# Another order of the first three batch steps, and of two tile turns, in a cross-attention and sparse FFN kernel

## The reference, cut to what matters

```python
# x: (32, 64, 512), ctx: (32, 64, 512)
# attention, 8 heads of 64, on the normalized x; the context is both key and value
qh = softmax(einsum('bcn,oc->bon', q, Wq).reshape(b, 8, 64, n), axis=-2) * 64 ** -0.5
kh = softmax(einsum('bcn,oc->bon', k, Wk).reshape(b, 8, 64, n), axis=-1)
vh = einsum('bcn,oc->bon', v, Wv).reshape(b, 8, 64, n)
context = einsum('bhdn,bhen->bhde', kh, vh)
out = einsum('bhde,bhdn->bhen', context, qh)
out = einsum('bcn,oc->bon', out.reshape(b, 512, n), Wo) + bo
x = x + out / max(norm(out, axis=1), 1e-12) * g * sqrt(64)
# feed-forward on the normalized rows of x
inter = xf @ c1_w.T @ c2_w.T                       # 1792 columns, 56 blocks of 32
idx = argmax over each block                       # one row of w1 and w2t for each block
h = relu(einsum('bkm,bm->bk', w1[idx], xf))
x = x + einsum('bk,bkm->bm', h, w2t[idx])
```

## Time and profile before

| | |
|---|---|
| median of 3 runs | 772.08 us (771.66 to 772.16) |
| the profiled execution | 771.59 us, span 769.8 us |
| PE busy | 753.8 us (98%) |
| DVE busy | 612.9 us (80%) |
| POOL busy | 476.9 us (62%) |
| ACT busy | 405.0 us (53%) |
| mean granted PE clock | 0.993 |

### The profile page before, as it was taken

How to read it: one execution, slowest core, us unless ns; L and a number is a source line. 1 busy time by engine, 2 the same in 40 slices (tenths; PEclk the granted TensorE clock), 3 DMA queues, 4 the chain that set the end, 5 groups by cost and what they waited for, 6 DMA issues and landing times.

```text
span 769.8 us, 13685 instructions
## 1 busy us (share of the span) xinstructions
PE 753.8 (98%) x4792; PEld 552.9 (72%) x4792; DVE 612.9 (80%) x936; ACT 405.0 (53%) x804; POOL 476.9 (62%) x547
## 2 busy tenths in 40 slices
PE   7979999999999999999999999999999999999998
PEld 6556655665665666666578888888888888888886
DVE  6879999999999999999866667776668766677763
ACT  4869999999999999999721111111111111111110
POOL 3699999988888889977444335544345443355431
PEclk8999999999999999999999999999999999999999
DMA  6143343333323333221111011110111100111000
GB/s 164 49 118 108 103 117 110 102 94 98 101 77 100 93 86 116 85 83 28 35 28 38 5 41 42 42 42 8 34 42 42 42 25 17 42 42 42 27 2 27
DMA packets 30531, 48.04 MB, mean 62 GB/s; under 512 B 4736, under 2 KB 13568, under 8 KB 30464
## 3 DMA queue, kind: packets, MB, share of 16 engines
q1 hardware_dynamic: 29808, 46.45, 20.3%
q10 hardware_dynamic: 656, 0.72, 0.3%
HBM read 38.77 MB, written 8.39 MB: 61 GB/s over the span
## 4 chain that ended last, share of the span: by engine, by line
PE 78%; POOL 13%; DVE 4%; ACT 2%; issue 2%; DMA 1%; DVEq 0%; SPq 0%; POOLq 0%; ACTq 0%
PE po L954 20%; PE slot L926 19%; PE po L1044 9%; PE turn L1029 5%; PE turn L1012 5%; POOL Q L415 5%; PE slot L1070 4%; PE slot L1084 4%; PE turn L939 3%; POOL weights_lo L366 2%; PE slot L911 2%; PE po L1055 2%; POOL c_low L400 2%; POOL x_low L356 1%; POOL weights_hi L364 1%
## 5 line engine op out<-in xcount | busy, mean ns | idle before, releaser
L325 POOL TENSOR_TENSOR E<-E,rank 128x256 bf16<-128x256 bf16 (+1 forms) x64 | 66.6, 1041 | 157.2 <-DVE E L498 157.2
L415 POOL TENSOR_TENSOR Q<-Q,qrec 128x1024 f32<-128x1024 f32 x64 | 121.2, 1903 | 37.7 <-DVE qrec L629 37.3
L1044 PE MATMUL po<-E,ctxT 128*64 128x512 f32 x256 | 116.7, 598 | 0.0
L1047 PE MATMUL po<-QT,G 128*64 128x512 f32 x256 | 116.7, 598 | 0.0
L734 ACT ACTIVATE wk_hi<-turn 128x256 fp32r<-128x256 f32 (+1 forms) x32 | 15.7, 490 | 155.3 <-PE turn L939 155.3
L926 PE MATMUL slot<-weights_hi,c_high 128*128 128x512 f32 (+1 forms) x256 | 96.9, 378 | 0.0
L926 PE MATMUL slot<-weights_hi,c_low 128*128 128x512 f32 (+1 forms) x256 | 94.3, 368 | 0.0
L926 PE MATMUL slot<-weights_lo,c_high 128*128 128x512 f32 (+1 forms) x256 | 94.3, 368 | 0.0
L773 ACT ACTIVATE E<-slot,neg_kmax 128x512 f32<-128x512 f32 x128 | 86.2, 685 | 12.1 <-DVE neg_kmax L615 11.9
L954 PE MATMUL po<-weights_hi,x_high 128*128 128x512 f32 x224 | 88.1, 393 | 0.0
L581 DVE TENSOR_REDUCE qmax<-slot 128x16 f32<-128x1024 f32 x64 | 75.4, 1218 | 14.1 <-PE slot L1084 14.1
(11 more groups left out here) (118 smaller groups left out, 1717.6 us busy)
## 6 DMA issues: line engine op xcount, KB each, us to landing
c_in<-in_ctx SPq DMA_DIRECT2D x64, 128.0 KB, 2.6
x_in<-in_x SPq DMA_DIRECT2D x64, 128.0 KB, 2.5
stage<-in_ffn_w SPq DMA_DIRECT2D x32, 225.0 KB, 2.6
attn_out<-po_sb SPq DMA_DIRECT2D x32, 128.0 KB, 2.3
ctxT<-in_ctxT SPq DMA_DIRECT2D x31, 128.0 KB, 2.1
attn<-attn_out SPq DMA_DIRECT2D x8, 256.0 KB, 3.0
x<-in_x SPq DMA_DIRECT2D x8, 256.0 KB, 2.8
E<-attn_out SPq DMA_DIRECT2D x8, 256.0 KB, 3.8
```

The source lines that it names most:

```text
L415: nc.gpsimd.tensor_tensor(half, half, qrec[1 - par][:, s, :].unsqueeze(2).broadcast_to([P, HALF, D]), ALU.mult).then_inc(q_scaled, 1)
L1044: nc.tensor.matmul(po[0:C, :], ctxT[1 - par][:, m, :], E[1 - par][:, :, m * P:(m + 1) * P], start=(m == 0), stop=(m == NT - 1)).then_inc(p ...
L1047: nc.tensor.matmul(po[C:P, :], G[:, m, :], QT[m][:], start=(m == 0), stop=(m == HT - 1)).then_inc(out_mm, 1)
```

## The change

It does seven things.

1. POOL, step 2: `bias(3, 1)` moves from the end of step 1 to behind the split of the context, and the two weight pieces move behind the scaling of the queries.
2. DVE, step 0: `statistics(1, 1)` moves from ahead of `max_k(1)` to behind `shift_q(0)`.
3. DVE, step 0 to 1: `sum_q(0, 0, 0)` moves behind the first `max_k(0)` of step 1.
4. ACT, step 0: `exp_q(0)` moves ahead of the copies, `norm_x` behind `copy_e(2)`, `exp_q(1)` ahead of `copy_e(3)`.
5. PE, step 0: 4 more matmuls on zeros behind `fold_vo`, and 5 between `queries(0)` and `queries(1)`.
6. PE: `turn_back(0)` moves from the end of step 30 to behind the keys of step 31.
7. `turn_x(0)` writes the bank `turn[1]` in place of `pre`, and waits for three copies of step 31, not four; ACT's and DVE's readers of it take the bank as an argument.

```diff
@@ gpsimd, step
-                    split_items()
+                    if known == 2:
+                        bias(3, 1)
+                    else:
+                        split_items()
...
                     if known == 1:
                         bias(2, 0)
-                    if known > 0:
+                    elif known == 2:
+                        split_items()
+                    if known > 1:
                         bias(g + 2, par)
@@ vector, step
                     max_k(0)
+                    if known == 1:
+                        sum_q(0, 0, 0)
                     invert_q(0)
                     if known == 0:
                         split_first_x()
-                        statistics(1, 1)
                     max_k(1)
...
                     if known == B:
-                        xT_rest(0, 0)
+                        xT_rest(0, 0, turn[1])
...
                     if known == 0:
                         shift_q(0)
+                        statistics(1, 1)
                     max_q(1)
...
-                    sum_q(g, par, 0)
+                    if known != 0:
+                        sum_q(g, par, 0)
@@ scalar, step
                     if known == B:
-                        xT_round(0, 0)
+                        xT_round(0, 0, turn[1])
...
+                    if known == 0:
+                        exp_q(0)
                     copy_e(0)
                     copy_e(1)
-                    if known == 0:
-                        norm_x()
                     copy_q(0)
                     copy_q(1)
                     copy_e(2)
-                    if known == 1:
+                    if known in (0, 1):
                         norm_x()
-                    exp_q(0)
+                    if known != 0:
+                        exp_q(0)
...
+                    if known == 0:
+                        exp_q(1)
                     copy_e(3)
-                    exp_q(1)
+                    if known != 0:
+                        exp_q(1)
@@ tensor
-                def turn_x(a, par):
+                def turn_x(a, par, bank):
                     pe.wait_ge(x2_normed, a + 1)
                     pe.wait_ge(added, a + 1)
                     if a == 0:
-                        pe.wait_ge(q_copied, HT * (B - 1))
+                        pe.wait_ge(q_copied, HT * (B - 2) + 3)
                     for m in range(MT):
-                        last = nc.tensor.transpose(pre[:, m * P:(m + 1) * P], work[:, m * P:(m + 1) * P], ident[:])
+                        last = nc.tensor.transpose(bank[:, m * P:(m + 1) * P], work[:, m * P:(m + 1) * P], ident[:])
                     last.then_inc(x_turned, 1)
...
+                def zeros(n):
+                    for _ in range(n):
+                        nc.tensor.matmul(turn[2][:, 0:P], QT[0][:, 0:P], QT[0][:, 0:P], start=True, stop=True)
...
                     if known == 0:
                         fold_vo()
+                        zeros(4)
                         pe.wait_ge(rest_in, 32)
+                    if known == B - 1:
+                        turn_back(0)
                     for m in range(HT):
                         products(m)
                     if known == B:
                         hide(0, 0, 0)
                     queries(0)
+                    if known == 0:
+                        zeros(5)
                     queries(1)
...
-                    if known == B - 2:
-                        turn_back(0)
                     if known == B - 1:
-                        turn_x(0, 0)
+                        turn_x(0, 0, turn[1])
```

More of the change, by code:

```diff
@@ L476, in normalize, with xT_rest @@
                                             ALU.mult).then_inc(x2_normed, 1)
-                def xT_rest(a, par):
+                def xT_rest(a, par, bank):
                     dve.wait_ge(xT_hi_done, a + 1)
-                    nc.vector.tensor_tensor(xT_lo[par], pre[:].rearrange("p (m n) -> p m n", m=MT),
+                    nc.vector.tensor_tensor(xT_lo[par], bank[:].rearrange("p (m n) -> p m n", m=MT),
                                             xT_hi[par].bitcast(fp32), ALU.subtract).then_inc(xT_lo_done, 1)
@@ L555, in tile @@
                     if not last:
-                        xT_rest(p + 1, 1 - par)
+                        xT_rest(p + 1, 1 - par, pre)
                     gate(3)
@@ L703, in keep_turned, with xT_round @@
                     nc.scalar.activation(turned_attn[:], bank[:], ACT.Copy).then_inc(attn_kept, 1)
-                def xT_round(a, par):
+                def xT_round(a, par, bank):
                     act.wait_ge(x_turned, a + 1)
@@ L708, in xT_round @@
                         act.wait_ge(h_mm, NC * (a - 1))
-                    nc.scalar.activation(xT_hi[par], pre[:].rearrange("p (m n) -> p m n", m=MT),
+                    nc.scalar.activation(xT_hi[par], bank[:].rearrange("p (m n) -> p m n", m=MT),
                                          ACT.Copy).then_inc(xT_hi_done, 1)
@@ L739, in tile @@
                     if not last:
-                        xT_round(p + 1, 1 - par)
+                        xT_round(p + 1, 1 - par, pre)
                         z_copy(p + 1)
@@ L970, in tile @@
                     if not last_tile:
-                        turn_x(p + 1, 1 - par)
+                        turn_x(p + 1, 1 - par, pre)
                     down(1)
@@ L989, in step @@
                         pe.wait_ge(idle_set, 1)
-                        for _ in range(12):
-                            nc.tensor.matmul(turn[2][:, 0:P], QT[0][:, 0:P], QT[0][:, 0:P], start=True, stop=True)
+                        zeros(12)
                         return
```

## The result

The changed kernel takes 766.68 us (median of 4 runs, 766.28 to 767.20), the kernel before 772.12 (4 runs, 771.66 to 772.44). The ratio is 0.993, with a 95% interval from 0.9913 to 0.9948: 5.4 us faster, where 4.4 were forecast. The profiled execution took 767.2 (span 765.4), 4.4 less than the 771.59 of the one before.

The account below looks back on a forecast made before the run. POOL was taken to bound steps 3 to 11, with PE following at full clock from 160 to 340 us. Start 3.3 plus passage 1.1 made 4.4 us off the 772.08 median: 767.7, range 766.3 to 769.7.

Parts of the forecast that it names:

- passage: Around step 31: moving turn_back(0) and waiting for the third copy makes turn_x(0) 1.1 us earlier, bounds 0.5 to 1.3.
- x_low of step 1: POOL in step 1: x_low starts at 18.6 us instead of 19.86.
- POOL's run begins: POOL's unbroken run into step 2 begins at 29.6 us, not 32.90, 3.3 us earlier.
- PE's hole in step 3: PE's 4.25 us idle stretch in step 2 goes; PE waits some 3.6 us in step 3 instead.
- POOL waits in step 4: POOL's 0.36 us wait for a late second reciprocal comes again, in step 4 instead of step 3.
- Step 0: Zeros take 1.1 and 1.4 us at no cost, PE's clock stays at 2.4 GHz, norm_x and its rounding end 1.25 earlier.
- Steps 1 and 2: turn_q(0) of step 1 comes 2.5 us earlier; POOL does not wait for reciprocals, though up to 0.5 may be lost.
- The clock case: Rival: PE's clock falls in step 0 despite the zeros, all behind is 1.5 us later, 769.2 us; chance 0.14.
- The zeros in the way: Rival: slow zeros hold up the queries in step 0, only the passage gains, 771.0 us; chance 0.08.
- The slower rival: Rival: PE's hole moved to step 3 brings the lower clock there, 7.3 us over forecast, 775.0 us; chance 0.03.
- costs nothing while POOL bounds: Step 3: PE's moved wait of some 3.6 us before the query turns was priced at nothing.
- the price of nothing: POOL's query scaling beside new DVE work: no added cost, since all 64 scalings last 1899 to 1907 ns.

Follow-up runs that it names:

- repeated trace: The changed kernel timed and traced once more with nothing altered; median 766.49 us, against 772.22 for the kernel before in the same group.
- start only: The changed kernel with the parts on the passage put back as before; median 767.68 us, against 772.22 for the kernel before.
- passage only: The kernel before with only the change's parts on the passage added; median 770.96 us, against 772.22 for the kernel before.
- no zeros: The changed kernel without the nine added matmuls on zeros in step 0; median 768.18 us, against 772.59 for the kernel before.
- DVE, ACT old: The changed kernel with DVE's and ACT's orders in steps 0 and 1 undone, zeros kept; median 767.85 us, against 772.80 for the kernel before.

## Why the prediction came out right, and where its steps were off

The median fell at 766.68, in the range and 1.0 under the forecast of 767.7. The mechanism was right: an earlier run of POOL and an earlier passage, with the clock that held in step 0. The signs came out too: clock 1.00 from 10 to 20 us, no wait for a reciprocal in steps 1 and 2, and the hole on PE moved to step 3. The chain of waits is POOL's from 64 to 140 us; ahead of that, in the profiled execution, it runs over DVE's reciprocals of step 4, which the prediction had as a wait of 0.36 only. That the profiled pair differs by the forecast 4.4 to the digit is luck: `turn_x(0)` is 3.96 earlier net of the first DMA, the late landing takes 0.87 back, and the 1.30 that before lost in its tile stage, a term the sum does not have, add to it.

| step | forecast, us earlier | measured, net of the first DMA |
|---|---|---|
| x_low of step 1 | 1.3 | 1.52 |
| POOL's run begins | 3.3 | 3.8 (x_low of step 3) |
| PE's hole in step 3 | 3.6 long | 3.42 |
| POOL waits in step 4 | 0.36 | 1.31, 0.45 (repeated trace), 0 (`start only`) |
| passage | 1.1 | 1.13 |
| `turn_x(0)` | 4.4 | 3.96, 4.83 (repeated trace), both against the first trace of before |
| `start only`, by medians | 3.3 | 4.5 |

**Step 0** went as the prediction had it: zeros at 1.16 and 1.38 us (forecast 1.1 and 1.4), clock 1.00. The term was 0.25 too small. **Steps 1 and 2**: no wait on a reciprocal on POOL, as said; x_low of step 2 follows that of step 1 by 10.73, forecast 11.0. These two make 3.8 out of 3.3.

**The reason given for that term was wrong in one place.** "The bias of x(3) is no longer ahead of x_low(2), so POOL's unbroken run begins at 29.6": the run begins within 0.26 us of there with POOL's old order too. I took the statistics of x(3) to stay at 32.9, but their wait is an effect of DVE being behind; they move with everything else. What carries most of the gain is DVE's and ACT's order and the clock that holds; beside them POOL's order is worth 0.25 at x_low of step 3.

**The clock case** was priced at 1.5 and measures 1.56 in the trace, 1.3 by medians. **The zeros in the way** fell. **The slower rival** was the right place and the wrong size: the lower clock behind the moved hole lasts some 6 us in the worst of these traces and costs POOL 1.31, where that rival had 7.3 over the forecast. The sentence that the hole "costs nothing while POOL bounds" did not hold: where the clock fell behind it, it cost 0.5 and 1.4 us at x_low of step 5 (59.99 and 60.90 against 59.50). The prediction had 0.36 of that as a wait in step 4.

**The passage** was right in sum and in cause, 0.63 and 0.50 from its two parts.

The scaling's length did not change with its new neighbours, over all 64:

```profile
L418 POOL TENSOR_TENSOR Q<-Q,qrec x64: 1897/1903/1907, 22.3 to 380.8; 128x1024 f32<-128x1024 f32 x64
```

DVE's work beside it is nearly all maxima, sums, statistics and reciprocals, which read one tile each. So the row bears out the price of nothing, but it does not test the rule that the prediction cites, whose condition is a two-port mode or two SBUF inputs; "for every overlap" said more than that rule does.

What stays open: `start only` measures 4.5 by medians, and its trace shows 3.8 at x_low of step 3. The kernel before waited 0.36, 0.34 and 1.73 us (`passage only`, same start) for reciprocals behind its own hole in step 2, where `start only` waited for none, so its lead over the first trace of before is 4.2 at x_low of step 5 and still 4.2 at `turn_x(0)`. The kernels with the old start lost another 0.5 to 1.3 us in the tile stage. But that trace is the fastest of six executions (767.01; the slowest took 769.05), and no run separates what the others lost.

## What to carry to other kernels

In a start where several engines wait for each other in turn, the worth of the parts does not add up: undo one at a time from the full change and also try each alone, since here the zeros were worth 1.3 us or 2.6 depending on the order beside them. Hold each trace against the other executions of its kernel before you explain it: here one in which the clock fell once more made a part look worthless that brings 2.6 us by medians. A hole that moves off the path can still cost through the clock behind it; filling it with idle matmuls, or feeding the waiting engine first, took back 1.4 to 2.8 us here. And at a handover from one bounding engine to the next it matters which work the next engine got early: an order that cost nothing while POOL bounded was worth 1.1 us where PE takes over.

## What the runs showed that I had not expected

Behind the same idle stretch of PE (3.38 to 3.43 us) the eight turns took 1.97, 1.55, 1.09, 1.95, 1.97, 1.09 and 1.27 us in seven traces, so the granted clock fell at once in some, within or behind the turns in others, and in `start only` not at all (1.00 from 50 to 62 us). I had cited the Trainium skill, TensorE: Matmul & The Clock Gate, Part 1, for a point of change that differs from run to run; these traces agree, for the fall of the clock as well. In `no zeros` 1.60 us of idle time before queries(1) went with 0.55 from 14 to 20 us, while in `DVE, ACT old`, where zeros stood ahead of it, 1.13 us left it at 1.00, and 1.48 us in its next step went with 0.57 from 26 to 30 us. The first context's transfer let its reader start anywhere from 5.39 to 6.57 us in these 14 traces, in either order of the two kernels, so two single traces are best compared from the first landing on.
